# Window-attention kernel: scores by quadrants of TensorE, masks as matmuls, and all four quarters of an image's masked keys held at once

## What is computed

```python
def _mhsa(x, w_qkv, b_qkv, w_o, b_o, mask):       # x: windows of 64 tokens, 8 heads of 16
    qkv = x @ w_qkv + b_qkv
    ...
    scores = jnp.einsum('bqhd,bkhd->bhqk', q, k) / jnp.sqrt(jnp.float32(hd))
    if mask is not None:
        scores = scores + mask[:, None, :, :]
    attn = jax.nn.softmax(scores, axis=-1)
    out = jnp.einsum('bhqk,bkhd->bqhd', attn, v).reshape(B, S, D)
    return out @ w_o + b_o

y = _mhsa(windows(x_norm), ..., None)             # 16 windows of 8 x 8 per image
ys = roll(reverse(y), (-4, -4))
ys = _mhsa(windows(ys), ..., mask)                # the same weights, shifted windows, with mask
x = x + roll(reverse(ys), (4, 4))
t = t + mixture_of_experts(graph_attention(layernorm(t), edge_index))   # 4 experts, top 2
```

## Time and profile before

| | |
|---|---|
| median of 3 runs | 8315.46 us (8314.64 to 8325.83) |
| the profiled execution: its own time | 8316.28 us |
| its span in the profile | 8314.6 us |
| mean granted clock of TensorE | 0.687 |
| busy in the span: VectorE / TensorE / GpSimd / ScalarE | 5201.6 / 4440.4 / 4861.2 / 2132.3 us |
| attention stage | from 0 to about 2300 us |

### The profile page before, as it was taken

The page is one execution under the profiler, slowest core; times in us unless marked ns, Lnnn a source line. Parts: engine busy times, 40 slices in busy tenths (PEclk is TensorE's granted clock), DMA queues, the critical chain, the costliest instruction groups (busy, mean ns, idle before and its releaser), DMA issues. The chain is left out here.

```text
span 8314.6 us, 101072 instructions
## 1 busy us (share of the span) xinstructions
PE 4440.4 (53%) x29005; PEld 2290.4 (28%) x29005; DVE 5201.6 (63%) x15789; ACT 2132.3 (26%) x3826; POOL 4861.2 (58%) x5216
## 2 busy tenths in 40 slices
PE   5889888989834445344443535445353444535200
PEld 3555555555511212122121212212121121212100
DVE  9999888988945455454545545454554545445368
ACT  4666666666510101001010100101010010101034
POOL 2221111111167777777777777777777777777573
PEclk9999999999855656556565655656565565656555
DMA  1121111111111111111111111111111111111267
GB/s 47 45 54 49 48 48 49 49 49 47 54 40 43 32 43 32 32 43 32 43 32 43 32 32 43 32 43 32 37 37 32 43 32 42 32 35 39 79 194 254
DMA packets 537622, 419.47 MB, mean 50 GB/s; under 512 B 177554, under 2 KB 450498, under 8 KB 536642
## 3 DMA queue, kind: packets, MB, share of 16 engines
q1 hardware_dynamic: 323058, 323.88, 12.0%
q0 software_dynamic: 147552, 56.96, 7.0%
q10 hardware_dynamic: 66560, 33.56, 1.4%
HBM read 203.65 MB, written 176.72 MB: 46 GB/s over the span
## 5 line engine op out<-in xcount | busy, mean ns | idle before, releaser
L1321 POOL DMA_INDIRECT edge_G<-node_rows,edge_src x4352 | 4159.5, 956 | 1326.3 <-issue 1326.3
L1358 PE MATMUL edge_cbank<-edge_ohh,edge_ohl 128*128 128x256 bf16 x4096 | 1417.4, 395 | 2951.5 <-DVE edge_ohh L1491 2878.4
L1358 PEld LDWEIGHTS edge_cbank<-edge_ohh,edge_ohl 128*128 128x128 bf16 x4096 | 427.5, 104 | 3934.8 <-DVE edge_ohh L1491 3758.9
L1491 DVE TENSOR_SCALAR edge_ohh<-edge_iob,edge_dlf 128x256 bf16<-128x256 bf16 x4096 | 1193.6, 298 | 0.0
L561 POOL TENSOR_SCALAR attn_nw<-attn_mv 128x8 f32<-128x8 f32 x64 | 89.8, 1403 | 1814.4 <-DVE attn_mv L979 1814.3
L1490 DVE TENSOR_SCALAR edge_ohl<-edge_iob,edge_dlf 128x128 bf16<-128x128 bf16 x4096 | 1084.1, 265 | 14.8 <-DVE edge_dlf L1484 14.5
L1338 ACT ACTIVATE edge_hid<-edge_hbank,edge_b1c 128x512 f32<-128x512 f32 x512 | 351.6, 687 | 2498.2 <-PE edge_hbank L1365 2498.2
L1449 DVE COPY edge_O<-edge_O 128x24 f32<-128x24 f32 x64 | 12.4, 193 | 1533.2 <-DMA edge_G<-node_rows,edge_src 1533.2
L1501 DVE TENSOR_TENSOR edge_yo<-edge_ybank,edge_b2r 128x512 f32<-128x512 f32 x256 | 176.9, 691 | 946.9 <-PE edge_ybank L1374 946.9
L1341 ACT ACTIVATE edge_w<-edge_w 128x272 f32<-128x272 f32 x64 | 27.5, 429 | 2405.3 <-DVE edge_w L1463 2405.3
L859 PE MATMUL attn_score<-attn_km,attn_qT 128*64 128x512 f32 x2048 | 537.2, 639 | 176.0 <-DMA attn_km<-attn_kT 98.0
(11 more groups left out here) (239 smaller groups left out, 6424.5 us busy)
## 6 DMA issues: line engine op xcount, KB each, us to landing
edge_G<-node_rows,edge_src POOLq DMA_INDIRECT x4352, 2.4
expert_out<-edge_yo SPq DMA_DIRECT2D x64, 1024.0 KB
comb_ye<-expert_out SPq DMA_DIRECT2D x32, 2048.0 KB, 11.8
state_rows<-edge_O SPq DMA_DIRECT2D x64, 816.0 KB, 3.7
attn_km<-attn_kT SPq DMA_DIRECT2D x2048, 16.0 KB, 1.8
attn_xin<-in_x SPq DMA_DIRECT2D x32, 512.0 KB, 4.1
attn_xres<-in_x SPq DMA_DIRECT2D x32, 512.0 KB, 5.6
x_rows<-attn_x SPq DMA_DIRECT2D x32, 512.0 KB, 3.4
```

The costliest lines, as they stand in the source:

```text
L1321: pool.indirect_dma_start(G[b][:, t, :], None, node_rows, bass.IndirectOffsetOnAxis(ap=src[b][:, t:t + 1], axis=0)).then_inc(s_g[b][2 * t ...
L1358: pe.matmul(cbank[b][:, 0:HI], ohl[:, t % RING, :], ohh[:, t % RING, :], start=(t == 0), stop=(t == HC - 1)).then_inc(s_ohp, 1)
L1491: dve.tensor_scalar(ohh[:, t % RING, :], iob[:, :], dlf[:, 1, t:t + 1], None, ALU.is_equal).then_inc(s_oh, 1)
```

## The change

Four things are changed together.

1. `score_bank` becomes [128, 2, 512] with the first index a for the half of the heads instead of the stream: bank a holds heads 4a to 4a + 3 of both streams, 256 columns each. The rows of heads 4a to 4a + 3 are the partitions 64a to 64a + 63, so a window's scores become two matmuls that contract over 64 rows each and have 256 columns. `S` and `mx` get the same order.
2. `km` holds all four quarters (and for each head slot both a head of the lower and one of the upper half of the partitions, so that its size stays). `own_rows` waits for the scores of the image before only. Quarter 1 is issued right behind quarter 0 at the end of the step before, for A, then for B.
3. The masks are bf16 tiles in the order of `km`, and TensorE adds them: a matmul of a bf16 identity (`ones`, cut to 64 x 64) with the mask, broadcast over four heads, accumulates onto the scores. The mask is per window (e), not per pair. VectorE's addition is gone.
4. The planner's constants: SLOT_US 8.05 for 8.4, and no 0.7 us for masked slots.

```diff
-KRING = 2
-SETUP = 11
+SETUP = 8
...
-        masks = sb("masks", [P, 3, WTOK])
+        masks = sb("masks", [P, 3, WTOK], BF16)
+        ones = sb("ones", [P, P], BF16)
...
-        km = [sb(f"km{s}", [P, KRING, HEADS, QWIN, WTOK]) for s in range(2)]
+        km = [sb(f"km{s}", [P, QUARTERS, HEADS // 2, QWIN, WTOK]) for s in range(2)]
...
-        S = [sb(f"S{i}", [P, 2, HEADS, WTOK]) for i in range(RING_S)]
-        mx = sb("mx", [P, PAIRS, 2, HEADS])
+        S = [sb(f"S{i}", [P, 2, 2, HEADS // 2, WTOK]) for i in range(RING_S)]
+        mx = sb("mx", [P, PAIRS, 2, 2, HEADS // 2])
...
-        SLOT_US = 8.4
+        SLOT_US = 8.05
...
-            busy = (2.5 + 0.7 * (mask_of(j) is not None) if two else 1.5) + 0.8
+            busy = (2.5 if two else 1.5) + 0.8
...
-        def mask_of(j):
-            row, right = j // 2 == WGRID - 1, j % 2 == 1
+        def mask_of(j, e):
+            below, right = j // 2 == WGRID - 1, j % 2 == 1 and e == 1
...
             def own_rows(s, m, q):
-                if q >= KRING or m > 0:
-                    sp.wait_ge(s_sc, (m + LAG[s]) * PAIRS + 2 * (q - KRING) + 2)
+                if m > 0:
+                    sp.wait_ge(s_sc, (m - 1 + LAG[s]) * PAIRS + 2 * q + 2)
                 for head in range(HEADS):
-                    sp.dma_start(km[st][lo:lo + HDIM, r, head, :, :]
+                    sp.dma_start(km[st][lo:lo + HDIM, q, head % (HEADS // 2), :, :]
...
-                for s in streams(n):
-                    own_rows(s, n - LAG[s], 1)
                 if 0 < n + 2 < IMAGES:
                     load_x(n + 2)
...
                     if active(f"{s}k0", n):
-                        own_rows(s, n - LAG[f"{s}k0"], 0)
+                        for q in range(2):
+                            own_rows(s, n - LAG[f"{s}k0"], q)
...
+                halves = [slice(a * P // 2, (a + 1) * P // 2) for a in range(2)]
+                out = [score_bank[e * WTOK:(e + 1) * WTOK, a, st * BANK // 2:(st + 1) * BANK // 2] for e in range(2) for a in range(2)]
+                mask = [mask_of(j, e) if s == "B" else None for e in range(2)]
                 for e in range(2):
                     w = (2 * j + e) % PAIRS
-                    last = pe.matmul(score_bank[e * WTOK:(e + 1) * WTOK, st, :], qT[st][h][:, w * WTOK:(w + 1) * WTOK],
-                                     km[st][:, q % KRING, :, (2 * j + e) % QWIN, :], start=True, stop=True)
+                    for a in range(2):
+                        last = pe.matmul(out[2 * e + a], qT[st][h][halves[a], w * WTOK:(w + 1) * WTOK],
+                                         km[st][halves[a], q, :, (2 * j + e) % QWIN, :], start=True, stop=mask[e] is None)
+                for e in range(2):
+                    if mask[e] is not None:
+                        for a in range(2):
+                            last = pe.matmul(out[2 * e + a], ones[halves[a], halves[a]],
+                                             masks[halves[a], mask[e], :].unsqueeze(1).to_broadcast([P // 2, HEADS // 2, WTOK]),
+                                             start=False, stop=True)
...
-                if hi == 2 and mask_of(j) is not None:
-                    b = score_bank[:, 1, :].rearrange("p (h k) -> p h k", h=HEADS)
-                    dve.tensor_tensor(b, b, masks[:, mask_of(j), :].unsqueeze(1).to_broadcast([P, HEADS, WTOK]), ALU.add
-                                      ).then_inc(s_mask, 1)
-                    masked[0] += 1
-                    dve.wait_ge(s_mask, masked[0])
```

More of the change, by code:

```diff
@@ L327, in attention @@
         s_tn = sem("s_tn")
-        s_km = [[sem(f"s_km{s}{r}") for r in range(KRING)] for s in "ab"]
+        s_km = [[sem(f"s_km{s}{r}") for r in range(QUARTERS)] for s in "ab"]
         s_kz = sem("s_kz")
@@ L375, in spare @@
             two = LAG["B"] <= n < IMAGES
-            busy = (2.5 + 0.7 * (mask_of(j) is not None) if two else 1.5) + 0.8
+            busy = (2.5 if two else 1.5) + 0.8
             busy += {4: 3.6, 6: 3.2, 7: 1.8}.get(j, 0.0)
             return SLOT_US - (0.0 if two else 1.5) - busy
-        def mask_of(j):
-            row, right = j // 2 == WGRID - 1, j % 2 == 1
-            return {(False, False): None, (False, True): 0, (True, False): 1, (True, True): 2}[(row, right)]
+        def mask_of(j, e):
+            below, right = j // 2 == WGRID - 1, j % 2 == 1 and e == 1
+            return {(False, False): None, (False, True): 0, (True, False): 1, (True, True): 2}[(below, right)]
         turns, turn_tasks, transfers, sort_operations = place_sort(spare, PAIRS)
@@ L448, in own_rows @@
             def own_rows(s, m, q):
-                st, h, r = STREAM[s], q // 2, q % KRING
+                st, h = STREAM[s], q // 2
                 if q % 2 == 0:
                     wait_free(sp, f"{s}k{h}", m)
-                if q >= KRING or m > 0:
-                    sp.wait_ge(s_sc, (m + LAG[s]) * PAIRS + 2 * (q - KRING) + 2)
+                if m > 0:
+                    sp.wait_ge(s_sc, (m - 1 + LAG[s]) * PAIRS + 2 * q + 2)
                 c = (q % 2) * QWIN * WTOK
@@ L459, in own_rows @@
                     lo = head * HDIM
-                    sp.dma_start(km[st][lo:lo + HDIM, r, head, :, :].rearrange("p w k -> p (w k)"),
-                                 kT[st][h][lo:lo + HDIM, c:c + QWIN * WTOK]).then_inc(s_km[st][r], 16)
+                    sp.dma_start(km[st][lo:lo + HDIM, q, head % (HEADS // 2), :, :].rearrange("p w k -> p (w k)"),
+                                 kT[st][h][lo:lo + HDIM, c:c + QWIN * WTOK]).then_inc(s_km[st][q], 16)
             sp.wait_ge(s_kz, 3)
@@ L595, in queries_or_keys @@
                     else:
-                        for r in range(KRING):
-                            act.wait_ge(s_km[st][r], KM_DONE * (2 * m - 1 + h))
+                        for q in range(2 * h, 2 * h + 2):
+                            act.wait_ge(s_km[st][q], KM_DONE * m)
                 dst, col = ((qT, 0), (kT, 1))[task[1] == "k"]
@@ L721, in _ @@
                         lo, hi = span(k)
-                        t = S[i % RING_S][:, lo:hi, :, :].rearrange("p s h k -> p (s h k)")
+                        t = S[i % RING_S][:, :, lo:hi, :, :].rearrange("p a s h k -> p a (s h k)")
                         act.activation(t, t, ACT.Exp, scale=SCALE).then_inc(s_exp, 1)
@@ L868, in turn @@
                     st = STREAM[s]
-                    src = S[j % RING_S][:, st, :, :].rearrange("p h k -> p (h k)")
                     for g in range(GROUPS):
-                        last = pe.transpose(turn_bank[:, st, g * P:(g + 1) * P], src[:, g * P:(g + 1) * P], ident[:, :])
+                        a, h = divmod(2 * g, HEADS // 2)
+                        src = S[j % RING_S][:, a, st, h:h + 2, :].rearrange("p h k -> p (h k)")
+                        last = pe.transpose(turn_bank[:, st, g * P:(g + 1) * P], src, ident[:, :])
                 last.then_inc(s_pt, 1)
@@ L890, in _ @@
             for n in steps:
+                if n == LAG["B"]:
+                    pe.wait_ge(s_cv, SETUP)
                 for j in range(PAIRS):
@@ L1089, in less_maximum @@
                 lo, hi = span(n)
-                both = score_bank[:, lo:hi, :].rearrange("p s (h k) -> p (s h) k", h=HEADS)
-                rows = (hi - lo) * HEADS
-                top = mx[:, j, lo:hi, :].rearrange("p s h -> p (s h)")
+                scores = score_bank[:, :, lo * BANK // 2:hi * BANK // 2].rearrange("p a (g k) -> p a g k", k=WTOK)
+                top = mx[:, j, :, lo:hi, :].rearrange("p a s h -> p a (s h)")
                 dve.wait_ge(s_sc, k + 1)
@@ L1095, in less_maximum @@
                     dve.wait_ge(s_pt, k + 1 - RING_S)
-                if hi == 2 and mask_of(j) is not None:
-                    b = score_bank[:, 1, :].rearrange("p (h k) -> p h k", h=HEADS)
-                    dve.tensor_tensor(b, b, masks[:, mask_of(j), :].unsqueeze(1).to_broadcast([P, HEADS, WTOK]), ALU.add
-                                      ).then_inc(s_mask, 1)
-                    masked[0] += 1
-                    dve.wait_ge(s_mask, masked[0])
-                dve.tensor_reduce(top, both, AX_X, ALU.max).then_inc(s_mx, 1)
+                dve.tensor_reduce(top, scores, AX_X, ALU.max).then_inc(s_mx, 1)
                 dve.wait_ge(s_mx, k + 1)
-                dve.tensor_tensor(S[j % RING_S][:, lo:hi, :, :].rearrange("p s h k -> p (s h) k"), both,
-                                  top.unsqueeze(2).to_broadcast([P, rows, WTOK]), ALU.subtract).then_inc(s_sub, 1)
+                dve.tensor_tensor(S[j % RING_S][:, :, lo:hi, :, :].rearrange("p a s h k -> p a (s h) k"), scores,
+                                  top.unsqueeze(3).to_broadcast([P, 2, (hi - lo) * HEADS // 2, WTOK]), ALU.subtract).then_inc(s_sub, 1)
             for n in steps:
```

11 lines of the change are left out of this document (3 added, 8 removed).

## The result

The changed kernel takes 8373.3 us (median of 6 runs, 8349.5 to 8381.5) against 8320.1 (8310.5 to 8325.8) for the kernel before: ratio 1.0061, 95% interval 1.0047 to 1.0074. It is slower by about 50 us, where 117 us less was forecast.

A forecast was written before the change was run, and what follows sets the result against it. The attention stage was taken as VectorE-bound, with TensorE late in some slots and a DMA. 3.8 x 30 = 115 us, 4 with B alone and 4 from the tail less roundings: about 117 saved, 8200 us; range 8140 to 8285.

The forecast's parts named there:

- the 1.0 predicted: TensorE's scores of a slot by four overlapping quadrants: 1.0 us, saving 0.86 a slot, 6.9 a step.
- rival 2: Program order limits overlap of score matmuls: nine steps, 1.93 us a slot, no gain from halves; 8302 us, chance 0.10.
- Chain 5-0: Node-feature store follows ScalarE's slot 5 copy; B's quarter 0 behind it becomes 24th copy, landing 2.6 us after B's present score start.
- Chain 2-4: Load of x waits for slot 2's normalisation; quarter 2 queues behind it, delaying B's slot 4 scores; predicted to stay.
- slots 0 to 2: Reduce to reduce, 16.2 us, VectorE-bound; less one mask, 15.5.
- slots 2 to 4: Reduce to reduce, 16.8 us; normalisation 0.9 earlier and B's scores 0.4 shorter make 15.5.
- slot 4 to 5: Reduce to reduce, 8.35 us; less mask 0.7 and VectorE's wait 1.0, making 6.8.
- slot 5 to 0: Reduce to reduce, 24.25 us; VectorE needs 22.9, but the DMA floor is 24.1; gain 0.1.
- Rival 1: TensorE stops some 2.5 us for B's quarter 0, halving slot 0's clock; 80 us saved, 8236 us, chance 0.15.
- 3.6 and 0.6 less 0.3: Gain per step: 3.6 in the step shown, some 0.6 for larger mean waits, less 0.3 for slot 0's halved clock.
- 4 and 4: Gains outside the two-stream steps: 4 us in steps with B alone, 4 us from the tail.
- serial pieces: Score pieces run one after another: sixteen passes, 3.4 us a slot; 8515 us, slower, chance 0.07.

The follow-up runs named there:

- B's quarter 0 first: Changed kernel with the end-of-step copies ordered A's quarter 0, B's quarter 0, A's quarter 1, B's quarter 1: 8239.3 us, 0.9879 of the kernel before.
- both reorderings: Changed kernel with B's quarter 0 ahead of A's quarter 1 and quarter 2 ahead of the loads of x: 8082.5 us, 0.9689 of the kernel before.
- work in the stops: Changed kernel with six extra useless f32 matmuls on TensorE in slots 0 and 4, before the key-copy wait: 8258.2 us, 0.9923 of the kernel before.
- quarter 2 ahead of the loads: Changed kernel with quarter 2 of A and B issued ahead of the two loads of x: 8168.7 us, 0.9797 of the kernel before.
- quarter 2's place alone: Kernel before with quarter 2 issued ahead of the loads of x and nothing else: 8225.4 us, 0.9870 of the kernel before.
- the halves: Kernel before with scores by halves of the rows: alone 8245.4 us, 0.9913; with quarter 2 also ahead of the loads of x 8192.7 us, 0.9827.
- the masks: Kernel before with only the masks moved to TensorE, as 512-column bf16 matmuls on 128 rows per window: 8329.0 us, 1.0010 of the kernel before.
- the masks put back: Changed kernel with both reorderings and the masks added by VectorE again: 8196.1 us, 0.9828 of the kernel before.

## Why the prediction was wrong

**Right in it.** The scores' 16 records and the turns: B's 8 records to the transposes take 0.60 us (1190.28 to 1190.88), a full slot 0.93 to the mask (1200.24 to 1201.17), near the 1.0 predicted with the turns behind them. The first row below is TensorE between 1200.2 and 1200.4, the second between 1200.7 and 1200.85, where the second and the third group run:

```profile
1200.24 0.45 PE L862 MATMUL attn_score<-attn_km,attn_qT 64*64 64x256 f32 x4
...
1200.51 0.61 PE L862 MATMUL attn_score<-attn_km,attn_qT 64*64 64x256 f32 x8
```

The records start four at a time, in four groups (1200.24, 1200.51, 1200.72, 1200.94): the quadrants overlap, and the staircase of nine starts that rival 2 asks for is not there. That rival's working takes the two passes of a matmul to be issued one behind the other; a record does not tell its matmul or its pass, and within a group the starts follow each other by 7 ns, so the traces do not show whether program order as such is broken. The mask adds 0.2 us before the transposes (0.15 taken). VectorE's work fell by 107 us (103.8 of masks). Chain 5-0's floor was 17.6 us from the store to the last landing, and B's scores started 17.9 us after it. Chain 2-4 stayed.

**Wrong: the sum behind these chains.** The change that was predicted (for step 17) against the means of steps 3 to 30, from reduce to reduce:

| part, us | predicted change | before | changed | B's quarter 0 first | both reorderings |
|---|---|---|---|---|---|
| slots 0 to 2 | -0.7 | 16.6 | 17.8 | 15.6 | 15.7 |
| slots 2 to 4 | -1.3 | 17.9 | 18.4 | 17.0 | 15.4 |
| slot 4 to 5 | -1.55 | 8.7 | 8.6 | 8.4 | 6.4 |
| slot 5 to 0 | -0.15 | 24.2 | 25.1 | 23.9 | 22.1 |

- The step that failed first is "slots 0 to 2, 16.2 us, VectorE-bound: less one mask, 15.5": 0.7 less was predicted, 1.2 more measured. I asked of B's late quarter 0 only when the reduce of slot 0 could start, and found 0.1 us of gain. TensorE's whole list for slot 0 starts behind B's scores too, and it is the longest of the step: TensorE is busy for 7.7 us in it with both reorderings, and for 7.5 us in the next longest. From A's scores of slot 0 to the scores of slot 1 the changed kernel takes 13.0 us in the mean, and 8.0 with B's quarter 0 first. At half clock it took 10.0 us from B's scores in the step shown; in the next, at full clock and with two pieces of the sort (which 6 of the 30 steps have in slot 0), 9.3. I had counted on VectorE bounding there, with slack on TensorE.
- "Chain 2-4 with the normalisation earlier by the shorter scores" has the wrong sign. The normalisation stands behind ScalarE's copy of the turned scores, so behind TensorE, whose scores of slot 2 started 4.4 us after VectorE's subtraction instead of 2.5. The shorter scores were outrun by slot 0's lateness, and the load of x went later: 21.2 us after the reduce of slot 0 in the mean, where it was 19.4 before and is 17.7 with B's quarter 0 first. The two chains that I priced apart are in series: removing slot 0's wait took 1.4 us off slot 4's.
- "Slot 4 to 5: less mask 0.7 and the wait 1.0" did not come, and not because of slot 0: the part is still 8.4 us with B's quarter 0 first. Slot 5's wait, which I held to be covered by the shorter scores, was 2.1 us (1.2 before). It hangs on the clock behind the stop in slot 4: with work in the stops the part is 6.7 us, as predicted (6.8), and with quarter 2 ahead of the loads 6.4.
- The stop in slot 0 and its clock were a rival at 0.15 (8236) and 0.3 us a step in the forecast. Rival 1 named the mechanism and the place. It had the wrong size: it took 1.4 us a step off the saving, 1.3 of them in slot 0, and nothing for the slots behind. B's quarter 0 first is worth 1.8 points, 5.0 us for each of the 30 steps. With work in the stops the kernel gains 115 us, 3.8 us a step, slots 0 and 4 together.

With B's quarter 0 first the change saves 1.2%, 101 us of 8320, where 117 was forecast; so in total most of what the sum missed is this one stop. Its own adding up is loose too: 3.6 and 0.6 less 0.3 are 3.9 us a step, not 3.8, and 3.8 x 30 with 4 and 4 are 122 us, not 117. That decides nothing.

The rival that ended on the slower side, serial pieces, is refuted; the kernel became slower by the mechanism of another rival. 0.17 of the chances lay outside the range, all of it for causes that did not occur.

Taken apart: both reorderings are worth 3.7 points of the ratio in the changed kernel; without its stops the change gives 3.1% over the kernel before, of which 1.3 points are had by quarter 2's place alone, 0.4 more by the halves (0.9870 to 0.9827), and 1.4 by the masks. The shares hold in this order: by themselves the halves gave 0.9 and the masks nothing. The version with both reorderings beats both kernels.

Open: how the loss of slot 0 divides between the stop and the clock over the whole step, since no run filled slot 0 only. Within slots 0 to 2 the work in the stops brings 17.8 us to 16.3, and no stop 15.6, so there the clock is the larger part.

## What to carry to other kernels

A transfer issued early costs what stands behind it in its queue: ask of each DMA that is moved which copy is now the 24th and who needs that one first. Price a new wait by everything that its engine does next, up to the next chain that starts from that engine, and at the clock that the engine will have after the stop. An edit that takes work off an engine is worth its full price only where that engine is the last to arrive; taking the masks off VectorE was worth nothing in one place and 115 us in the other.

## What the runs showed of the hardware

- Four quadrants of 64 x 64 ran f32 matmuls at once: 16 records of 256 columns in about 0.93 us, starting four at a time, where eight of 512 columns took 1.87.
- TensorE's stop of 1.83 us in slot 4 of the kernel before was followed by 3.3 us at 1.2 GHz, that of 2.92 us in slot 0 of the changed kernel by 6.8; behind a stop of 2.50 us a step later the transposes ran at full clock (1.09 us; rows below). Useless matmuls in the stops raised the granted clock from 0.90 to 0.98 and made the kernel 1.4% faster than the changed one.

```profile
1260.66 0.66 PE L862 MATMUL attn_score<-attn_km,attn_qT 64*64 64x256 f32 x8 [2.50 <-DMA attn_km<-attn_kT]
1261.25 1.09 PE L881 MATMUL attn_turn<-attn_ident,attn_S 128*128 128x128 f32 x8
...
1269.93 1.09 PE L862 MATMUL attn_score<-attn_km,attn_qT 64*64 64x256 f32 x16
```

- A low clock alone says nothing. With the masks put back VectorE bounds: the clock was 0.93, lower than in the slower kernel before (0.95), and VectorE waited 0.4 us a step before its reduces (window of that run):

```profile
150.00:2151.00 2001.00, 1705.17 (x21076) 1192.94 (x21074) 1929.54 (x2908) 1361.82 (x2419) 404.80 (x538) 0.93 0.19 52
```
